# Three reorderings in a two-layer attention and feed-forward kernel: a product ahead of a weighing, turns behind an expansion, one wait for each last scatter

## The reference

```python
def _act_quant(a):
    scale = QB / jnp.clip(jnp.max(jnp.abs(a), axis=-1, keepdims=True), 1e-05)
    return jnp.clip(jnp.round(a * scale), -QB, QB) / scale
...
# the quantised layer, 2048 hidden columns
h = _rmsnorm(x, norm_w)
gv = _bitlinear(h, w_gv)
value, gate = jnp.split(gv, 2, axis=-1)
h = value * jax.nn.silu(gate)
return x + _bitlinear(h, w_out)
...
# the last block: each expert's rows are gathered, computed and added back
xg = xpad[buf]
mid = silu(xg @ w_gate[e]) * (xg @ w_up[e])
eout = (mid @ w_down[e]) * wbuf[..., None]
y = zeros.at[buf.reshape(-1)].add(eout.reshape(-1, h))[:T]
```

## Time and profile before

| | |
|---|---|
| median of three runs | 1034.89 us |
| the profiled execution | 1035.11 us |
| its span, first to last instruction | 1033.1 us |
| TensorE clock granted, mean over the span | 0.998 |
| PE busy | 1016.7 us, 98% |
| VectorE (DVE) busy | 695.6 us, 67% |
| ScalarE (ACT) busy | 598.9 us, 58% |
| GpSimd (POOL) busy | 282.2 us, 27% |
| PE's part of the chain that ended last | 76% |

### The profile page before, as it was taken

How to read it: one execution, slowest core, us unless ns; L and a number is a source line. 1 busy time by engine, 2 the same in 40 slices (tenths; PEclk the granted TensorE clock), 3 DMA queues, 4 the chain that set the end, 5 groups by cost and what they waited for, 6 DMA issues and landing times.

```text
span 1033.1 us, 16275 instructions
## 1 busy us (share of the span) xinstructions
PE 1016.7 (98%) x5715; PEld 803.6 (78%) x5738; DVE 695.6 (67%) x1371; ACT 598.9 (58%) x953; POOL 282.2 (27%) x444
## 2 busy tenths in 40 slices
PE   9999999999999999999999999999999999999996
PEld 6888888876455555578888888888888999999996
DVE  6757555538999998678777775677724666666662
ACT  6766788737898998874333344111203466666662
POOL 1022222125655553110000034100010154555542
PEclk9999999999999999999999999999999999999999
DMA  6693666522001000201111342302052588888863
GB/s 231 238 334 114 184 184 197 161 72 84 21 21 32 22 21 1 86 29 62 62 62 51 103 128 87 117 11 81 2 196 105 203 233 226 233 247 247 234 157 47
DMA packets 50339, 127.29 MB, mean 123 GB/s; under 512 B 5856, under 2 KB 9952, under 8 KB 49504
## 3 DMA queue, kind: packets, MB, share of 16 engines
q1 hardware_dynamic: 39248, 97.79, 28.2%
q0 software_dynamic: 10448, 27.58, 11.5%
q10 hardware_dynamic: 576, 1.05, 0.3%
HBM read 98.02 MB, written 28.38 MB: 122 GB/s over the span
## 4 chain that ended last, share of the span: by engine, by line
PE 76%; DVE 1%; issue 0%; POOL 0%; ACT 0%; DVEq 0%; ACTq 0%; POOLq 0%
PE bank L54 18%; PE bank L56 17%; PE bank L55 17%; PE bank L1475 10%; PE bank L1496 5%; PE bank L2422 1%; PE bank L1487 1%; PE bank L1556 1%; PE bank L1574 1%; PE bank L1505 1%; PE bank L1543 0%; PE bank L2409 0%; PE bank L2392 0%; PE bank L2393 0%; PE bank L1462 0%
## 5 line engine op out<-in xcount | busy, mean ns | idle before, releaser
L1475 PE MATMUL bank<-w,f_qT 128*128 128x512 bf16 x496 | 116.1, 379 | 2.6 <-DVE f_h L1771 1.7
L2244 POOL DMA_INDIRECT out<-e_y,scatter_idx x32 | 69.0, 2157 | 110.3 <-ACT e_y L2351 90.0
L1475 PEld LDWEIGHTS bank<-w,f_qT 128*128 128x128 bf16 x512 | 48.4, 98 | 52.0 <-issue 2.0
L2228 POOL DMA_INDIRECT e_xg<-xn_rows,gather_idx x32 | 32.3, 1009 | 166.1 <-DVE gather_idx L2630 99.1
L2282 ACT ACTIVATE s_m_h<-s_mid 128x512 fp32r<-128x512 f32 (+1 forms) x24 | 15.2, 632 | 107.4 <-DVE s_mid L2640 59.7
L2748 DVE TENSOR_TENSOR e_mid<-bank,e_sil 128x256 f32<-128x256 f32 (+1 forms) x47 | 19.7, 420 | 59.9 <-ACT e_sil L2321 49.3
L1496 PE MATMUL bank<-w,f_q2T 128*128 128x512 bf16 x249 | 57.3, 379 | 0.4
L1771 DVE SCALAR_TENSOR_TENSOR f_h<-bank,f_columns,f_sg 128x512 f32<-128x512 f32 x64 | 47.8, 749 | 12.9 <-ACT f_sg L1183 7.3
L54 PE MATMUL bank<-e_xT_h,e_wg_h 128*128 128x256 f32 (+1 forms) x192 | 55.3, 288 | 0.0
L56 PE MATMUL bank<-e_xT_h,e_wg_l 128*128 128x256 f32 (+1 forms) x192 | 54.1, 282 | 0.0
L55 PE MATMUL bank<-e_xT_l,e_wu_h 128*128 128x256 f32 (+1 forms) x192 | 54.1, 282 | 0.0
(11 more groups left out here) (466 smaller groups left out, 3310.6 us busy)
## 6 DMA issues: line engine op xcount, KB each, us to landing
wraw<-in_wffn SPq DMA_DIRECT2D x48, 512.0 KB, 4.1
e_raw_g<-in_ew_gate SPq DMA_DIRECT2D x16, 704.0 KB
e_raw_u<-in_ew_up SPq DMA_DIRECT2D x16, 704.0 KB
e_raw_d<-in_ew_down SPq DMA_DIRECT2D x16, 512.0 KB
sorted_y<-e_y SPq DMA_DIRECT2D x19, 256.0 KB
x_rows<-rows SPq DMA_DIRECT2D x16, 256.0 KB, 2.0
xn_rows<-a_work SPq DMA_DIRECT2D x16, 256.0 KB, 2.0
s_raw<-x_rows SPq DMA_DIRECT2D x16, 256.0 KB, 2.6
```

The source lines that it names most:

```text
L1475: ins = pe.matmul(bank[c % 2][:, :], qT[t % 2][:, k * P:(k + 1) * P], w_gv(k, col + c * 512), start=(k == 0), stop=(k == KD - 1))
L2228: gp.indirect_dma_start(xg[t][u][:, :], None, g.xn_dram, bass.IndirectOffsetOnAxis(g.gather_idx[:, slot:slot + 1], 0)).then_inc(e_arrived[ ...
L2244: gp.indirect_dma_start(io["out"], bass.IndirectOffsetOnAxis(g.scatter_idx[:, slot:slot + 1], 0), e_y[t][u][:, :], None, compute_op=ALU.ad ...
```

## The change

Three edits, none of which changes what is computed or how many instructions compute it.

1. `weigh` is split: the weighing stays `weigh`, and the row maximum behind it becomes `largest` on VectorE. Everywhere the two are still called one behind the other, except in step i = 1, which now runs product(1, 2), weigh(3), product(1, 3), largest(3), invert(3), reach(1).
2. In the last step of the quantised layer PE runs expand(15, 2), expand(15, 3), turn_q2(14), as in the other steps; behind the loop turn_x(13) stands ahead of contract(14). ScalarE runs silu(15, 2), silu(15, 3), normalise(13) and then both copies of tile 14's turned rows.
3. For the last expert POOL waits ahead of each scatter only for `e_y_ready[0]`, VectorE's half. VectorE in turn waits for `e_y_ready[1]`, ScalarE's half, before it computes its own.

```diff
--- before.py
+++ after.py
@@ -1327,13 +1327,11 @@
                         residual(i + 2)
                     if i > 1:
                         silu(i, 2)
-                        if i == TT - 1:
-                            copy_q2T(i - 1, 0)
                         silu(i, 3)
-                        if i == TT - 1:
-                            copy_q2T(i - 1, 1)
                     if have(i - 2):
                         normalise(i - 2)
+                copy_q2T(TT - 2, 0)
+                copy_q2T(TT - 2, 1)
                 query_weights()
                 split_x(TT - 3)
                 scale2(TT - 1, 0)
@@ -1619,13 +1617,11 @@
                     if have(i + 1):
                         turn_q(i + 1)
                     expand(i, 2)
-                    if i == TT - 1:
+                    expand(i, 3)
+                    if have(i - 1):
                         turn_q2(i - 1)
-                    expand(i, 3)
-                    if have(i - 1) and i < TT - 1:
-                        turn_q2(i - 1)
+                turn_x(TT - 3)
                 contract(TT - 2)
-                turn_x(TT - 3)
                 query(0)
                 turn_q2(TT - 1)
                 query(1)
@@ -1744,6 +1740,8 @@
                         v.wait_ge(q_ready, t - 1)
                     v.scalar_tensor_tensor(out=h[t % 2][:, :], in0=x1[t % 3][:, :], scalar=mv[t % 3][:, 0:1], in1=norm_b[:, :],
                                            op0=ALU.subtract, op1=ALU.mult).then_inc(h_ready, 1)
+
+                def largest(t):
                     v.wait_ge(h_ready, t + 1)
                     if t >= 3:
                         v.wait_ge(amax_ready, t - 2)
@@ -1906,11 +1904,13 @@
                 v.wait_ge(norm_in, 16)
                 statistics(0)
                 weigh(0)
+                largest(0)
                 negative(1)
                 features(1)
                 invert(0)
                 statistics(1)
                 weigh(1)
+                largest(1)
                 negative(2)
                 round_q(0)
                 features(2)
@@ -1919,6 +1919,7 @@
                 statistics(2)
                 features(3)
                 weigh(2)
+                largest(2)
                 round_q(1)
                 for i in range(TT):
                     if have(i - 1):
@@ -1941,18 +1942,25 @@
                         split_summary()
                     if have(i - 1):
                         low(i - 1)
+                    if i == 1:
+                        product(1, 2)
+                        weigh(3)
+                        product(1, 3)
+                        largest(3)
+                        invert(3)
+                        reach(1)
+                        continue
                     if i and have(i + 2):
                         weigh(i + 2)
+                        largest(i + 2)
                     if have(i - 2):
                         residual(i - 2)
                     product(i, 2)
                     if i == 0:
                         round_q(2)
-                    if i > 1 and have(i + 2):
+                    if i and have(i + 2):
                         invert(i + 2)
                     product(i, 3)
-                    if i == 1:
-                        invert(3)
                     if i == 0:
                         reach_half(0)
                         product(1, 0)
@@ -2237,9 +2245,10 @@
                 gp.drain()
             gp.sem_inc(y_free[1 - u], 1)
             for t in range(2):
-                gp.wait_ge(e_y_ready[u], i * 2 + (t + 1))
                 if e == E1 - 1:
                     gp.wait_ge(e_y_ready[0], 2 * PAIRS + (t + 1))
+                else:
+                    gp.wait_ge(e_y_ready[u], i * 2 + (t + 1))
                 slot = e * ST + t
                 gp.indirect_dma_start(io["out"], bass.IndirectOffsetOnAxis(g.scatter_idx[:, slot:slot + 1], 0), e_y[t][u][:, :], None,
                                       compute_op=ALU.add).then_inc(added[u], 16)
@@ -2778,6 +2787,7 @@
             v.wait_ge(y_free[1], PAIRS)
             for t in range(2):
                 v.wait_ge(e_o_ready[0], 2 * PAIRS + (t + 1))
+                v.wait_ge(e_y_ready[1], 2 * PAIRS - 1 + t)
                 weight = g.slot_weight[:, SLOTS - 2 + t:SLOTS - 1 + t]
                 v.tensor_scalar(e_y[t][1][:, HALF:D], last_banks[t][1][:, 0:HALF], weight, None, ALU.mult).then_inc(e_y_ready[0], 1)
```

## The result

| | before | changed |
|---|---|---|
| median of twelve executions | 1034.89 us | 1032.73 us (1032.26 to 1033.59) |
| ratio, 95% interval | | 0.9979 [0.9972, 0.9987] |
| profiled execution / its span | 1035.11 / 1033.1 us | 1032.70 / 1031.0 us |
| PE busy | 1016.7 us | 1016.8 us |

The direction was right. The lines of the changed program have moved: 1475 is now 1473, 1771 is 1769, 1496 is 1494, 1505 is 1503, 2244 is 2253, 2782 is 2792.

What follows compares the result with a forecast made beforehand. PE bounds the kernel, busy 1016.7 of 1033.1 us, so only its idle places can give time. Edits of 0.7 + 0 + 0.3 = 1.0 us off give a forecast of 1033.9 us, range 1032.9 to 1035.5.

Steps and rivals of the forecast that it cites:

- the three places named: PE's waits for product f_h (1.7 us) and for a_wq_l (0.6), and the scatters behind PE's last matmul.
- the new waits named: PE about 0.7 us before expand(3, 0), and for f_q2T or f_xn instead of a_wq_l; VectorE on POOL.
- Edit 1: Tile 1's step: expand(2, 0) 1.37 us earlier, PE then stalls 0.7 before expand(3, 0); keeps 0.7.
- The lead: PE's gain at tile 3, expected to carry through the other twelve tiles, since VectorE and ScalarE catch up.
- the hand-over: From VectorE's product end to PE's expansion start, taken as 0.35 us at expand(2, 0) and expand(3, 0).
- Rival C: POOL's round trip costs VectorE nothing, or product(2, 2) isn't waited for: edit 1 keeps 1.2 to 1.37; 1033.3 us; 12 in 100.
- Edit 2: Tile 14's turns: one wait of 0.6 to 0.7 us exchanged for two totalling 0.6 to 0.8; gain 0.
- Edit 3: Last expert's scatters: POOL gains 0.50 us, VectorE's later start loses 0.20; both scatters 0.3 earlier.
- Rival B: POOL's removed wait is free, VectorE's new one is not: edit 3 costs 0.2; 1034.4 us; 15 in 100.
- Rival A: Last expert's first scatter takes 2.90 us instead of 1.55, losing 1.05; 1035.2 us; 15 in 100.
- Rival D: VectorE 1 us late, or contract(14) waits longer: edits 1 and 2 give nothing; 1034.6 to 1035.2 us; 13 in 100.
- the gaps of edit 2: ScalarE's small gaps around tile 14's copies: 0.3 us gained if they fall well, 0.3 lost if badly.

Runs made afterwards that it cites:

- f1_turn_behind: The kernel before with only edit 2, but turn_x(13) left behind contract(14); 1036.61 us against 1035.03.
- f2_vector_waits: The kernel before with only VectorE's added wait for ScalarE's half, POOL keeping both waits; last scatter 1.80 us behind PE's last matmul, 1.58 before; no median given.
- g4_drain_earlier: The kernel before with a POOL drain also ahead of expert 13's scatters, as the last two experts have; 1035.24 us.
- f3_gather_behind: The kernel before with expert 15's gathers put behind expert 13's scatters instead of ahead; 1043.99 us.

## Why the prediction was right and wrong

- **Where the time goes: right but for one place.** The gain lies in the three places named, with the new waits named, and in one more that the prediction did not have: 0.17 at the attention's first `a_summ` matmuls, in every kernel with edit 2 (below). No wait appeared further on.
- **Edit 1, mechanism right, one term off.** reach(1) came 0.34 later relative to tile 0's turning (261.61 - 258.25 = 3.36 to 261.45 - 257.75 = 3.70; forecast 0.3). The lead was carried over twelve tiles. The mis-sized term is the hand-over: 0.35 forecast, 0.14 measured. Before, PE restarted 0.21 earlier than I read; and expand(3, 0) starts 0.14 behind its product, not 0.35. Of these only the second was in my sum at its wrong size, and 0.7 + 0.21 = 0.9 meets the 0.85. Rival C (1.2 and more) is out, since VectorE's 0.52 of idle time is there.
- **Edit 2: wrong, 0 forecast, 0.55 measured.** The step that failed is "silu(15, 3), at 426.72 before, starts at 425.83". PE's timeline of the kernel before, expand(15, 2) and expand(15, 3):

```profile
422.71 1.89 PE L1475 MATMUL bank<-w,f_qT 128*128 128x512 bf16 x8
...
425.33 1.89 PE L1475 MATMUL bank<-w,f_qT 128*128 128x512 bf16 x8
```

  silu(15, 3) started 426.72 - 425.33 = 1.39 behind its expansion, silu(15, 2) only 423.82 - 422.71 = 1.11. I moved the silu by the 0.89 of the turning alone. With turning and copy gone from ahead of it, it moved by 0.89 + 0.28 = 1.17: it is 424.19 - 421.35 = 2.84 behind expand(15, 2), where it was 4.01. ScalarE is continuous from there, so copy 0 (4.14 behind expand(15, 2), forecast 427.1 - 422.71 = 4.39), `contract(14)` (5.29, forecast 428.25 - 422.71 = 5.54) and the weights (5.95, forecast 6.2) all come 0.25 earlier than in my list. Where the 0.28 came from stays open. That a copy stands ahead on ScalarE and a turning on PE does not explain it, since silu(15, 0) has both ahead of it and starts 416.48 - 415.36 = 1.12 behind its expansion:

```profile
415.15 1.00 ACT L1199 ACTIVATE f_q2T<-bank 128x1024 bf16<-128x1024 bf16 x1
416.48 0.69 ACT L1183 ACTIVATE f_sg<-bank,f_columns 128x512 f32<-128x512 f32 x1 [0.32 <-issue]
```

  At query(0) the gain is 0.43, 0.25 from ScalarE and 0.18 from a shorter contraction: 3.27 from start to start ahead of a query (429.91 - 426.64), where I had twice 1.73. Most of the 0.18 is only how the first row is drawn, for the query's second matmul follows 0.42 behind its first, where it was 0.31 before; measured there the gain is 0.32. The rest comes later: 0.36 at the turning of tile 15 (434.62 - 422.71 = 11.91 before, 432.90 - 421.35 = 11.55 now), and 0.53 once the attention's first `a_summ` matmuls are under way (their first `mm3`: 454.30 - 422.71 = 31.59 before, 452.41 - 421.35 = 31.06 now). VectorE's `a_q_first` and that matmul, before and changed:

```profile
453.20 0.69 DVE L1837 TENSOR_TENSOR a_q_first<-f_sg,a_q_first 128x512 fp32r<-128x512 f32 x1 [0.70 <-ACT a_q_first L1238]
454.03 0.37 PE L1543 MATMUL bank<-a_summ,a_q_first 128*128 128x264 f32 x1
```

```profile
451.06 0.69 DVE L1835 TENSOR_TENSOR a_q_first<-f_sg,a_q_first 128x512 fp32r<-128x512 f32 x1 [0.70 <-ACT a_q_first L1238]
452.22 0.29 PE L1541 MATMUL bank<-a_summ,a_q_first 128*128 128x264 f32 x1
```

  Before, PE started 0.14 behind VectorE's end, the hand-over found at the expansions: it was waiting, though no wait is printed. With the change VectorE is through 0.47 earlier than PE gets there. That wait of about 0.17 was missing from my account, and it is the 0.10 that the table of stretches has behind its `a_summ` mark, together with some of the 0.45 ahead of it. I had allowed 0.3 to either side, too little for a sum of eight steps that leaned on one difference. That turn_x had to move was right: f1_turn_behind loses without it.
- **Edit 3: right.** VectorE later by 0.22 (0.20 forecast), POOL quicker by 0.50 (0.50 forecast), together 0.28 (0.3). Rival B is out: the removed wait was not free. The Trainium skill, VectorE: DVE Perf Modes, The DRAIN you can't avoid, has semaphores cost nothing extra between VectorE's own instructions, which no run here tests. It can't be carried to POOL, where the scatter behind two waits starts 0.78 after its last input and behind one wait 0.28.
- **Rival A: fell.** 1.55, not 2.90. **Rival D: fell**, edits 1 and 2 give 1.4.
- **Size.** 0.85 + 0.55 + 0.28 = 1.68 by stretches, 1.70 by the traces, 1.95 in the mean of three pairs of medians (2.16, 1.92, 1.78). Two pairs of equal kernels differ by -0.09 and +0.25, so the 0.25 between 1.70 and 1.95 is not told apart from chance. Of the miss of 1.2 us (1033.9 to 1032.73), 0.7 is my two mis-sized terms (1.7 less 1.0), and about 0.5 is left to chance in the first pair of medians. So even with every term right I would have forecast 1033.2, inside my range, and the measured median would still have been 0.5 below. The range allowed for the gaps of edit 2 and for rival C, but for none of this chance.

## What to carry to other kernels

Compare two profiles by stretches between marks that the change can't move; here that brought noise of 0.5 us down to 0.04 and priced edits that no interval could tell apart. Before a gap is priced from a row, count its matmuls: a row with x15 of 16 starts a matmul late. When a turn or any producer is moved behind other work, the work that fills the new wait (here `turn_x`) decides on the sign. A second wait in front of an indirect DMA is best given to an engine that waits more cheaply; here VectorE took it for 0.22, or 0.09 behind its product, instead of POOL's 0.50. And when an instruction has two lengths, look first at what the other engines do during it.

## What the runs showed of the hardware

- An indirect DMA on GpSimd starts 0.28 us after its last input when it has one wait ahead of it, and 0.78 when it has two, even where the other half was there 0.37 before (1024.88 and 1025.25 in the kernel before), or 0.59 before (f2_vector_waits).
- A scatter takes 1.55 to 1.6 us, but 2.72 to 2.91 when VectorE is in a 128x1408 product of two weight buffers as it starts; it then ends 1.44 to 1.52 behind VectorE's end (the kernel before, g4_drain_earlier, f3_gather_behind). Seen in every such row, tested only by the shift of 0.2 in g4_drain_earlier.
- The time from the program's start to the first turned tile of the quantised layer varied from 257.5 to 259.2 us between executions of nearly the same program, while the 768 us from there to the last scatter repeat within 0.04 for an equal program. The cause is open.
